# Scaling head 0's probabilities before head 1's decay on VectorE, and copying head 1's first transposes before y on ScalarE

## The chip, the cores and the metric

The kernel runs on one core of a Trainium2 chip (trn2). The metric is the device time of one execution in microseconds (us), given as the median of several runs. The profiled execution is one run of its own, and its span goes from the first to the last instruction.

## The reference

A batch of 8 sequences, each of 36 image tokens and 512 text tokens (548 rows of 192 values), goes through one layer: a normalised attention with decay in 3 heads of 64, and a mixture of 16 experts. Cut to what matters here:

```python
scores = jnp.einsum('blhe,bmhe->bhlm', q, k) / jnp.sqrt(jnp.float32(hd))
decay = jnp.where(mask, gammas[:, None, None] ** dclip, 0.0)   # 0 below the diagonal
weights = jax.nn.softmax(scores * decay[None], axis=-1)
o = jnp.einsum('bhlm,bmhe->blhe', weights, v)
o = (o - mean) / jnp.sqrt(var + GN_EPS)                        # per sequence and head
h = h + (o.reshape(B, L, D) * gn_weight + gn_bias) @ Wo.T
h = h + ffn(layernorm(h))                                      # router, top 8 of 16 experts
```

## The kernel before, in words

Each engine has its own program, written out by hand in the order in which it runs, and the programs meet only at semaphores. There is no scheduler. The attention part goes over the 8 sequences in a function `body(b, ...)` of each engine: b = 0, 1 and 7 are written out, b = 2 to 6 are a loop in hardware. The expert part, `STEPS` steps of up, gelu, weigh, round and down, follows it.

One iteration has three heads. A head passes through four engines. **TensorE** makes the scores (`scores`, L1178) in five row tiles, of which tiles 2 to 4 share PSUM bank 3. **VectorE** multiplies them with the decay table and takes the row maximum (`apply_decay`, L912), and hands the negated maxima on as `nm` (L918), first that of tile 0, after all five tiles those of the other four. **ScalarE** takes the exponentials from the scores `sc` to the probabilities `pr` (`exps`, L598), with the row sums, and an exponential of the maxima alone (`zero_score`, L595), which stands for the positions below the diagonal. VectorE makes the denominators (`den`, L925 and L927), their reciprocals (L929) and scales the five tiles of `pr` in place (`normalise`, L935; tiles of 580, 452, 324, 196 and 68 columns). TensorE transposes the scaled tiles (`probs_transpose`, L1316), in groups 0 to 3, ScalarE copies each group to `pt` (`pt_copy`, L516), and TensorE multiplies with the values (`attend`). Heads 0 and 2 use the buffers `sc[0]` and `pr[0]`, head 1 `sc[1]` and `pr[1]`. So head 1's decay and head 0's scaling touch different buffers.

TensorE's order around the change is: scores of head 1, `values` (the fifth and last tile of which is written to bank 3 and so waits for all of head 1's decay), transposes of head 0, `gn_sums` of the sequence before, `attend` of head 0, transposes 0 and 1 of head 1, scores of head 2, transposes 2 and 3 of head 1, `attend` of head 1.

ScalarE puts head 1's exponentials between its copies of the values, and copies head 0's groups 0 and 1 between the fourth and the fifth exponential. Later it makes y of the sequence before, which waits for coefficients that GpSimd computes (`gn_coefficients`, last instruction L465) from `gvar` (L960). VectorE gets at `gvar` after `gn_partial` (L943 to L950) and head 1's scaling.

**GpSimd** is waiting for `veps` (L828), the last step of the statistics of the next sequence, which VectorE computes between head 0's and head 1's decay. Then it computes `rstd` with a power (L425), two small instructions for `nmr` (L426, L428), and then splits a share of the weights w1: two casts (`w_hi`, L447) and two subtractions (`w_lo`, L450). In b = 7 it splits its share after `second_twice`, instead.

The waits that matter, as the code has them:

```python
# normalise (VectorE)
dve.wait_ge(exp_done, nth(b, H, hh + 1))
# values (TensorE), last tile
if I == NT - 1:
    pe.wait_ge(decayed, nth(b, NT * H, 2 * NT))
# attend (TensorE), before its first matmul
pe.wait_ge(pt_copied, nth(b, 4 * H, 4 * hh + 2))
# probs_transpose (TensorE), groups 2 and 3 of head 1
pe.wait_ge(pt_copied, nth(b, 4 * H, 4 * hh + 1))
# halve_w1 (GpSimd), after rstd_of(b + 1)
pool.wait_ge(ld_w1, nth(b, 16, 16))
```

Of the kernel before, what the change touches and what calls it, by code (L numbers as in the profile page):

```python
# [83 lines left out]
def width(t):  # L84
    return WIDTHS[t]
# [12 lines left out]
def nth(b, per, k):  # L98

    return b * per + k  # L100


def early_fusion(nc, patches, txt, tok_w, tok_b, gammas, gn_w, gn_b, attn_w, w1, w2, out):
# [9 lines left out]
    with ctx:  # L113
# [398 lines left out]
        def _(sc_eng):  # L512
# [90 lines left out]
            def pt_copy(b, hh, groups=(0, 1, 2, 3)):  # L603
                for g in groups:
                    a.wait_ge(pt_done, nth(b, 4 * H, 4 * hh + g + 1))
                    if g == 0:
                        last = copy(pt[:KEY_LAST, 0, :], ps[:KEY_LAST, 5, :])
                    elif g == 1:
                        copy(pt[:KEY_LAST, 1, 0:LAST], ps[:KEY_LAST, 4, 0:LAST])
                        last = copy(pt[:, 1, 64:64 + 3 * P], ps[:, 4, P:4 * P])  # L610
                    elif g == 2:
                        last = copy(pt[:, 2, :], ps[:, 5 if hh else 0, :])
                    else:
                        last = copy(pt[:, 3, 0:3 * P], ps[:, 4 if hh else 1, 0:3 * P])
                    last.then_inc(pt_copied, 1)
# [26 lines left out]
            def logits_exp(t):  # L642
                r = width(t) // SEG
                a.wait_ge(l_sub, t + 1)
                a.activation(lexp[:r, :, :], lsub[:r, :, :], ACT.Exp).then_inc(l_exp, 1)
# [8 lines left out]
            def body(b, tail, later, more):  # L654
                t = b - 1
                qk_round(b, (0,))
                if tail:
                    scale_probs(t)
                qk_round(b, (1, 2, 3))
                if tail:  # L660
                    pt_copy(t, 2)
                if not more:
                    second_norm(0)
                exps(b, 0)
                if tail:
                    o_copy(t, 1)
                if not more:
                    x2_round(0, 0, 4)
                    x2_round(0, 1, 5)
                exps(b, 1, (0,))  # L670
                v_copy(b, (0,))
                exps(b, 1, (1,))
                v_copy(b, (1,))
                exps(b, 1, (2,))
                v_copy(b, (2,))
                exps(b, 1, (3,))
                pt_copy(b, 0, (0, 1))
                exps(b, 1, (4,))
                pt_copy(b, 0, (2, 3))
                if more:  # L680
                    norm_apply(b + 1, rstd, nmr, ln1_rstd, xn, ln1_normed)
                else:
                    logits_exp(0)
                if tail:
                    y_round(t, 0)
                pt_copy(b, 1, (0, 1))
                if tail:
                    y_whole(t, 0)
                    y_round(t, 1)
                pt_copy(b, 1, (2, 3))  # L690
                if tail:
                    y_whole(t, 1)
                exps(b, 2, (0,))
                o_copy(b, 0)
                if more:
                    x_hi(b + 1, 0)
                    x_hi(b + 1, 1)
                    exps(b, 2, (1, 2, 3, 4))
                else:
                    comb_copy(0, 5)  # L700
                    exps(b, 2, (1, 2, 3, 4))
# [89 lines left out]
        def _(dve):  # L791
# [22 lines left out]
            def norm_stats(b, s6, m2, ve, signal):  # L814

                norm_parts(b, s6)
                dve.drain()
                norm_join(s6, m2, ve, signal)
# [79 lines left out]
            def apply_decay(b, hh):  # L898
                s = hh % 2
                for I in range(NT):  # L900
                    r, n = rows(I), L - P * I
                    if I <= 2:
                        dve.wait_ge(s_done, nth(b, 3 * H, 3 * hh + I + 1))
                        apart(dve, "dve")
                    dst, tab = sc[s][:r, OFF[I]:OFF[I] + n], decay[:r, hh, 0:n]
                    if I == 0:
                        dst, tab, src = two(dst), two(tab), ps[:, 0:2, 0:HALF]
                    elif I == 1:
                        src = ps[:, 2, 0:n]
                    else:  # L910
                        src = ps[:r, 3, S_AT[I]:S_AT[I] + n]
                    dve.tensor_tensor_reduce(out=dst, in0=src, in1=tab, scale=1.0 / 8, scalar=0.0 if I else NEG,  # L912
                                             op0=ALU.mult, op1=ALU.max,
                                             accum_out=mx[s][:r, I:I + 1]).then_inc(decayed, 1)
                    if I in (0, NT - 1):
                        dve.drain()
                        cols = slice(0, 1) if I == 0 else slice(1, NT)
                        dve.tensor_scalar(nm[s][:, cols], mx[s][:, cols], -1.0, None, ALU.mult).then_inc(nm_ready, 1)  # L918
# [118 lines left out]
            def body(b, tail, later, more):  # L1037
                t = b - 1
                if isinstance(b, int) and b == 0:
                    dve.wait_ge(ld_h, 16 * NT)  # L1040
                qk_rest(b, (0, 1, 2, 3))
                if not more:
                    second_norm(0)
                if isinstance(b, int) and b == 0:
                    dve.wait_ge(ld_decay, 16)
                    dve.wait_ge(consts, 3)
                apply_decay(b, 0)
                if more:
                    norm_stats(b + 1, st6, mv, veps, ln1_var)
                apply_decay(b, 1)  # L1050
                if not more:
                    x2_rest(0, 0, 4)
                    x2_rest(0, 1, 5)
                normalise(b, 0)
                if tail:
                    gn_partial(t)
                normalise(b, 1)
                if tail:
                    gn_variance(t)
                if not more:  # L1060
                    router_shift(0, 2)
                    router_top(0)
                    router_left(0)
                    router_weights(0)
                apply_decay(b, 2)
                if tail:
                    y_rest(t)
                if more:
                    x_ext(b + 1)
                    x_lo(b + 1, (0,))  # L1070
                    if tail:
                        add_attention(t, (6, 4, 5), (0,))
                    x_lo(b + 1, (1,))
                    if tail:
                        add_attention(t, (6, 4, 5), (1, 2))
                normalise(b, 2)
                if not more:
                    add_attention(t, (4, 3, 5))
# [514 lines left out]
```

## Time and profile before

| what | value |
|---|---|
| median of 3 runs | 849.03 us (848.9 to 854.23) |
| profiled execution | 850.09 us, its span 848.3 us |
| granted TensorE clock, mean | 0.983 of full |
| busy TensorE, VectorE, ScalarE, GpSimd | 805.3, 558.7, 508.2, 101.1 us |
| share of the span | 95%, 66%, 60%, 12% |

The attention part takes the first 320 us or so of the span. One iteration of the hardware loop takes 35.9 us. TensorE is busy for nearly all of both parts, so the time moves only where TensorE waits, or where it begins to.

### The profile page before, as it was taken

The page shows a single profiled execution, that of the slowest core. Times are in us where ns is not written, and L with a number is a line of the kernel's source. Part 1 is how long each engine was busy: PE and PEld are TensorE (multiplying, and loading weights), DVE is VectorE, ACT ScalarE, POOL GpSimd, SP SyncE. Part 2 cuts the span into 40 slices and gives each one's busy share as a digit, 9 for nine tenths or more (in the row PEclk, how much of TensorE's full clock was granted, in tenths as well). Part 3 has the DMA queues.
Part 4 walks back from the last instruction along what each step waited for, and adds up shares of the span by engine and source line. Part 5 has one row for each costly group of instructions (what it writes and reads, how often), then busy time and mean ns, then how long its engine had stood idle before and what let it go on. Part 6 is the DMA issues. An engine that isn't in the chain of part 4 may idle for free.

```text
span 848.3 us, 13687 instructions
## 1 busy us (share of the span) xinstructions
PE 805.3 (95%) x4336; PEld 678.4 (80%) x4336; DVE 558.7 (66%) x1559; ACT 508.2 (60%) x1134; POOL 101.1 (12%) x187
## 2 busy tenths in 40 slices
PE   6799999999999998799999999999999999999997
PEld 2677878797787876677888888888888888888886
DVE  5667677677767777565666666666666566666654
ACT  1367867778777774465555645556555556465443
POOL 2022020220202208300101001001010010000000
PEclk9689999999999999999999999999999999999999
DMA  7400010101103027213422324134133241241420
GB/s 221 152 19 17 5 40 0 38 0 38 38 0 93 1 60 208 79 50 93 120 63 71 106 62 133 41 85 123 53 96 91 68 128 47 80 96 61 113 56 18
DMA packets 44376, 60.77 MB, mean 72 GB/s; under 512 B 4018, under 2 KB 37762, under 8 KB 44322
## 3 DMA queue, kind: packets, MB, share of 16 engines
q1 hardware_dynamic: 44322, 60.10, 25.5%
q8 instruction: 27, 0.44, 0.2%
q14 instruction: 27, 0.22, 0.1%
HBM read 52.04 MB, written 8.05 MB: 71 GB/s over the span
## 4 chain that ended last, share of the span: by engine, by line
PE 61%; issue 26%; POOL 6%; POOLq 3%; DVE 2%; ACT 2%; DVEq 0%; ACTq 0%
PE ps L1178 58%; POOL w_lo L450 2%; POOLq L427 1%; POOL w_lo L482 1%; PE ps L1378 1%; POOLq L460 1%; POOLq L481 1%; POOL w_r L480 0%; PE ps L1316 0%; PE ps L1487 0%; ACT pt L516 0%; PE ps L1488 0%; DVE sc L912 0%; POOLq L448 0%; PE ps L1397 0%
## 5 line engine op out<-in xcount | busy, mean ns | idle before, releaser
L1089 DVE TENSOR_TENSOR act<-act,gate 128x480 f32<-128x480 f32 (+1 forms) x216 | 145.1, 672 | 120.0 <-ACT act L714 118.7
L1178 PE MATMUL ps<-x,w_hi 128*128 128x480 f32 (+1 forms) x648 | 217.4, 390 | 0.0
L714 ACT ACTIVATE act<-ps 128x480 f32<-128x480 f32 (+1 forms) x216 | 124.0, 574 | 125.9 <-PE ps L1178 125.7
L1178 PE MATMUL ps<-x,w_lo 128*128 128x480 f32 (+1 forms) x432 | 165.6, 383 | 0.0
L867 DVE TENSOR_TENSOR act_lo<-act,act_hi 128x480 fp32r<-128x480 f32 (+1 forms) x216 | 144.3, 668 | 0.1
L1178 PEld LDWEIGHTS ps<-x,w_hi 128*128 128x128 f32 x648 | 122.5, 189 | 19.8
L516 ACT ACTIVATE act_hi<-act 128x480 fp32r<-128x480 f32 (+1 forms) x216 | 130.8, 605 | 7.9 <-DVE act L1089 7.9
L1178 PEld LDWEIGHTS ps<-x,w_lo 128*128 128x128 f32 x432 | 81.8, 189 | 13.3
L1178 PE MATMUL ps<-act_hi,w_hi 128*128 128x480 f32 (+1 forms) x216 | 83.9, 388 | 6.6 <-DVE act_lo L867 6.6
L1178 PE MATMUL ps<-act_lo,w_hi 128*128 128x480 f32 (+1 forms) x216 | 83.8, 388 | 0.0
L1178 PE MATMUL ps<-act_lo,w_r 128*128 128x480 f32 (+1 forms) x216 | 83.0, 384 | 0.0
L1178 PE MATMUL ps<-act_hi,w_lo 128*128 128x480 f32 (+1 forms) x216 | 82.8, 384 | 0.0
L1178 PE MATMUL ps<-pt,v 68*128 68x512 f32 (+5 forms) x288 | 82.4, 436 | 0.0
L1178 PE MATMUL ps<-act_hi,w_r 128*128 128x480 f32 (+1 forms) x216 | 82.3, 381 | 0.0
L1178 PEld LDWEIGHTS ps<-pt,v 128*128 128x128 f32 (+1 forms) x288 | 49.0, 190 | 31.1 <-issue 21.6
L598 ACT ACTIVATE pr<-sc,nm 128x580 f32<-128x580 f32 (+4 forms) x120 | 66.8, 559 | 10.7 <-DVE nm L918 10.7
L912 DVE CUSTOM_DVE_ANT_0 sc<-ps,decay 128x548 f32<-128x548 f32 (+4 forms) x120 | 49.7, 458 | 35.5 <-PE ps L1178 33.3
L516 ACT ACTIVATE pt<-ps 128x384 f32<-128x384 f32 (+3 forms) x120 | 48.4, 466 | 23.8 <-PE ps L1316 23.6
L1316 PE MATMUL ps<-ident,pr 128*128 128x128 f32 (+1 forms) x360 | 47.2, 276 | 11.6 <-DVE pr L935 9.1
L425 POOL TENSOR_TENSOR rstdb<-vepsb,neg_half 128x4 f32<-128x4 f32 x9 | 12.2, 1353 | 364.9 <-DVE vepsb L989 364.9
L1178 PEld LDWEIGHTS ps<-act_hi,w_hi 128*128 128x128 f32 x216 | 40.5, 187 | 16.4 <-DVE act_lo L867 9.9
L1316 PEld LDWEIGHTS ps<-ident,pr 128*128 128x128 f32 (+1 forms) x360 | 39.1, 132 | 15.7 <-DVE pr L935 10.9
(173 smaller groups left out, 1318.1 us busy)
## 6 DMA issues: line engine op xcount, KB each, us to landing
gate<-comb_dram SPq DMA_DIRECT2D x112, 240.0 KB, 3.3
gate<-comb_dram SPq DMA_DIRECT2D x32, 256.0 KB, 3.7
w_raw<-w SPq DMA_DIRECT2D x16, 384.0 KB, 3.9
h_dram<-h SPq DMA_DIRECT2D x8, 384.0 KB
res<-h_dram SPq DMA_DIRECT2D x7, 360.0 KB, 4.5
out<-res SPq DMA_DIRECT2D x7, 360.0 KB, 3.2
h<-txt SPq DMA_DIRECT2D x3, 672.0 KB
decay_rows<-drow SPq DMA_DIRECT2D x1, 1014.0 KB, 8.0
```

Source lines behind the costliest of these rows:

```text
L425: pool.tensor_tensor(rs[:, :], ve[:, :], neg_half[:, 0:n], ALU.pow)
L427: pool.drain()
L450: last = pool.tensor_tensor(w1_lo[:, c, cols], w1_raw[:, c, :], w1_hi[:, c, cols], ALU.subtract)
L460: pool.drain()
L516: return a.activation(dst, src, ACT.Copy)
L598: last = a.activation(pr[s][:r, cols], sc[s][:r, cols], ACT.Exp, bias=nm[s][:r, I:I + 1], accum_out=row_sum[s][:r, I:I + 1])
L714: a.activation(act[j % 3][:, 0:n], ps[:, up_bank(j), 0:n], ACT.Gelu_apprx_tanh).then_inc(gelu_done, 1)
L867: return dve.tensor_tensor(dst, src, hi, ALU.subtract)
L912: dve.tensor_tensor_reduce(out=dst, in0=src, in1=tab, scale=1.0 / 8, scalar=0.0 if I else NEG, op0=ALU.mult, op1=ALU.max, accum_out=mx[s][ ...
L1089: dve.tensor_tensor(act[j % 3][:, 0:n], act[j % 3][:, 0:n], gate[e % 4][:, 0:n], ALU.mult).then_inc(gated, 1)
L1178: return pe.matmul(dst, w, x, start=start, stop=stop)
L1316: return pe.transpose(dst, pr[s][:, at:at + n], ident[:, :])
```

## The change

Two pieces of code are moved, and nothing is added or removed. On VectorE `normalise(b, 0)` stands before `apply_decay(b, 1)`. In b = 7 this also puts it before `x2_rest`. On ScalarE the copies of head 1's groups 0 and 1 stand before `y_round(t, 0)`, instead of behind it.

```diff
@@ -681,10 +681,9 @@
                     norm_apply(b + 1, rstd, nmr, ln1_rstd, xn, ln1_normed)
                 else:
                     logits_exp(0)
+                pt_copy(b, 1, (0, 1))
                 if tail:
                     y_round(t, 0)
-                pt_copy(b, 1, (0, 1))
-                if tail:
                     y_whole(t, 0)
                     y_round(t, 1)
                 pt_copy(b, 1, (2, 3))
@@ -1047,11 +1046,11 @@
                 apply_decay(b, 0)
                 if more:
                     norm_stats(b + 1, st6, mv, veps, ln1_var)
+                normalise(b, 0)
                 apply_decay(b, 1)
                 if not more:
                     x2_rest(0, 0, 4)
                     x2_rest(0, 1, 5)
-                normalise(b, 0)
                 if tail:
                     gn_partial(t)
                 normalise(b, 1)
```

All lines behind L684 are one lower in the changed kernel (L935 is L934 there) up to the second piece.

VectorE in the hardware loop, before, from the last step of the statistics on; `sc,mx<-ps,decay` is head 1's decay, of which the first tile and the maxima stand here, and `pr<-pr,inv_den` head 0's scaling:

```order
234 L828 TENSOR_SCALAR veps<-mv 128x5
235 L903 REGISTER_ALU
236 L912 ISA sc,mx<-ps,decay 128x548 [waits s_done]
237 L912 ISA mx 128x1
238 L918 TENSOR_SCALAR nm<-mx 128x1
```

The end of the decay follows eight rows further on, and only then head 0's scaling:

```order
247 L912 ISA sc,mx<-ps,decay 36x36
248 L912 ISA mx 36x1
249 L918 TENSOR_SCALAR nm<-mx 128x4
250 L923 ISA
251 L925 TENSOR_TENSOR den<-zero_score,lower_count 128x5 [waits exp_done]
252 L927 TENSOR_TENSOR den<-den,row_sum 128x5
253 L929 RECIPROCAL inv_den<-den 128x5
254 L935 TENSOR_SCALAR pr<-pr,inv_den 128x580
```

The same place in the changed kernel:

```order
234 L827 TENSOR_SCALAR veps<-mv 128x5
235 L922 ISA
236 L924 TENSOR_TENSOR den<-zero_score,lower_count 128x5 [waits exp_done]
237 L926 TENSOR_TENSOR den<-den,row_sum 128x5
238 L928 RECIPROCAL inv_den<-den 128x5
239 L934 TENSOR_SCALAR pr<-pr,inv_den 128x580
240 L934 TENSOR_SCALAR pr<-pr,inv_den 128x452
241 L934 TENSOR_SCALAR pr<-pr,inv_den 128x324
242 L934 TENSOR_SCALAR pr<-pr,inv_den 128x196
243 L934 TENSOR_SCALAR pr<-pr,inv_den 36x68
244 L902 REGISTER_ALU
245 L911 ISA sc,mx<-ps,decay 128x548 [waits s_done]
```

The wait for `exp_done` now stands directly behind the statistics, and the whole of head 1's decay is queued behind it and behind the eight instructions that follow it.

ScalarE in the written-out iteration b = 1, before, from the normalised x on (`y<-ot` and `ot<-ot` are y, `pt<-ps` the copies of head 1):

```order
95 L546 ACTIVATE xn<-h,nmr,rstd 36x192
96 L626 ACTIVATE y<-ot,gshift,gscale 128x548 [waits y_coeff]
97 L516 ACTIVATE pt<-ps 68x512 [waits pt_done]
98 L516 ACTIVATE pt<-ps 68x36 [waits pt_done]
99 L516 ACTIVATE pt<-ps 128x384
100 L626 ACTIVATE ot<-ot,gshift,gscale 128x548
```

And changed:

```order
95 L546 ACTIVATE xn<-h,nmr,rstd 36x192
96 L516 ACTIVATE pt<-ps 68x512 [waits pt_done]
97 L516 ACTIVATE pt<-ps 68x36 [waits pt_done]
98 L516 ACTIVATE pt<-ps 128x384
99 L626 ACTIVATE y<-ot,gshift,gscale 128x548 [waits y_coeff]
100 L626 ACTIVATE ot<-ot,gshift,gscale 128x548
```

The three copies no longer stand behind the wait for GpSimd's coefficients. The rest of both programs, and those of the other engines, are unchanged.

## Rows read from the trace of the kernel before

**Rows 1.** Waits of TensorE, 40 to 330 us: total us, times, longest us

```profile
PE ps L1316 <- DVE pr L935: 9.1, 7, 1.4
```

**Rows 2.** Timeline of TensorE, loop iteration b = 3: start us, us, ... [idle before]

```profile
156.60 1.83 PE L1316 MATMUL ps<-ident,pr 128*68 128x128 f32 x15 [1.34 <-DVE pr L935]
...
159.12 3.49 PE L1178 MATMUL ps<-pt,v 68*128 68x512 f32 x12
162.44 1.04 PE L1316 MATMUL ps<-ident,pr 128*68 128x128 f32 x8
...
165.01 1.01 PE L1316 MATMUL ps<-ident,pr 128*128 128x128 f32 x7
```

**Rows 3.** Timeline of VectorE, the same iteration

```profile
150.93 0.73 DVE L912 CUSTOM_DVE_ANT_0 sc<-ps,decay 128x548 f32<-128x548 f32 x1 [1.64 <-PE ps L1178]
...
153.46 0.87 DVE L918 TENSOR_SCALAR nm<-mx 128x4 f32<-128x4 f32 x1
154.24 0.15 DVE L925 TENSOR_TENSOR den<-zero_score,lower_count 128x5 f32<-128x5 f32 x1
...
154.97 1.57 DVE L935 TENSOR_SCALAR pr<-pr,inv_den 128x580 f32<-128x580 f32 x5
...
161.64 0.17 DVE L960 TENSOR_SCALAR gvar<-gvar 128x2 f32<-128x2 f32 x1
```

**Rows 4.** Timeline of ScalarE, the same iteration

```profile
149.86 0.19 ACT L598 ACTIVATION_READ_ACCUMULATOR pr<-sc,nm 36x1 f32 x1
...
151.95 0.78 ACT L598 ACTIVATE pr<-sc,nm 128x580 f32<-128x580 f32 x1 [1.34 <-DVE nm L918]
...
154.36 0.21 ACT L595 ACTIVATE zero_score<-nm 128x5 f32<-128x5 f32 x1 [0.18 <-DVE nm L918]
...
157.27 1.06 ACT L516 ACTIVATE pt<-ps 68x512 f32<-68x512 f32 x3 [0.20 <-PE ps L1316]
...
163.63 0.84 ACT L626 ACTIVATE y<-ot,gshift,gscale 128x548 fp32r<-128x548 f32 x1 [1.94 <-POOL gshift L465]
164.38 1.03 ACT L516 ACTIVATE pt<-ps 68x512 f32<-68x512 f32 x3
```

**Rows 5.** Timeline of GpSimd, the same iteration

```profile
149.37 1.19 POOL L425 TENSOR_TENSOR rstd<-veps,neg_half 128x5 f32<-128x5 f32 x1 [21.28 <-DVE veps L828]
...
150.87 0.20 POOL L428 TENSOR_TENSOR nmr<-nmr,rstd 128x5 f32<-128x5 f32 x1
151.15 0.95 POOL L447 CAST w_hi<-w_raw 128x384 f32 x2
152.31 1.99 POOL L450 TENSOR_TENSOR w_lo<-w_raw,w_hi 128x384 f32 x2 [0.21 <-issue]
```

**Rows 6.** VectorE grouped by shape, 118.9 to 120.7 us: busy us, mean ns | idle

```profile
L935 DVE TENSOR_SCALAR pr<-pr,inv_den 128x580 f32<-128x580 f32 x1 | 0.5, 523 | 0.1
...
L935 DVE TENSOR_SCALAR pr<-pr,inv_den 128x196 f32<-128x196 f32 x1 | 0.3, 316 | 0.0
```

**Rows 7.** VectorE grouped by shape, 317.4 to 320.3 us (head 2 of b = 7)

```profile
L935 DVE TENSOR_SCALAR pr<-pr,inv_den 128x196 f32<-128x196 f32 x1 | 1.1, 1078 | 0.0
```

**Rows 8.** VectorE grouped by shape, 44 to 50.2 us (b = 0)

```profile
L927 DVE TENSOR_TENSOR den<-den,row_sum 128x5 f32<-128x5 f32 x1 | 1.0, 1018 | 0.1
L935 DVE TENSOR_SCALAR pr<-pr,inv_den 128x580 f32<-128x580 f32 x1 | 0.9, 922 | 0.1
```

**Rows 9.** Timeline of GpSimd, expert part: a power like that of `rstd`

```profile
740.26 1.38 POOL L425 TENSOR_TENSOR rstdb<-vepsb,neg_half 128x4 f32<-128x4 f32 x1 [49.83 <-DVE vepsb L989]
```

**Rows 10.** VectorE grouped by shape, 739.5 to 742 us

```profile
L1089 DVE TENSOR_TENSOR act<-act,gate 128x480 f32<-128x480 f32 x2 | 1.3, 656 | 0.0
```

**Rows 11.** Page, part 5: the whole group of the same line: busy, mean ns | idle

```profile
L1089 DVE TENSOR_TENSOR act<-act,gate 128x480 f32<-128x480 f32 (+1 forms) x216 | 145.1, 672 | 120.0 <-ACT act L714 118.7
```

**Rows 12.** Timeline of VectorE, b = 7

```profile
294.69 0.73 DVE L912 CUSTOM_DVE_ANT_0 sc<-ps,decay 128x548 f32<-128x548 f32 x1 [2.68 <-PE ps L1178]
```

**Rows 13.** Timeline of ScalarE, b = 7

```profile
295.52 0.19 ACT L598 ACTIVATION_READ_ACCUMULATOR pr<-sc,nm 36x1 f32 x1
```

## The prediction

> **What bounds the kernel now.** I read the page first: TensorE is busy for nearly all of the span, so only its waits can be won. The list of waits, cut to the attention part, has one large entry: the transposes of head 0 wait for VectorE's scaling 7 times, 9.1 us in all [rows 1]. All numbers below are from the timelines of one iteration of the hardware loop, b = 3. The reader is to see three things there. TensorE idles 1.34 us ahead of the transposes [rows 2], because the scaling, which starts at 154.97, is queued behind head 1's decay [rows 3]. Head 0's exponentials were already done at 149.86 + 0.19 = 150.05 [rows 4], and VectorE idled 1.64 us before 150.93 [rows 3]. So the work could be done in the gap, in part. And GpSimd works exactly in that stretch: 149.37 to 154.30 [rows 5].
>
> **First edit, what it moves.** From the first `den` to the first `pr` it is 154.97 - 154.24 = 0.73 us, and the five scalings take 1.57 us: 2.30 us [rows 3]. Started at 150.09 (150.05 and 0.04 for the semaphore) they would end at 152.39, undisturbed. Head 1's decay then starts not at 150.93 but at about 152.38. Call its delay d; it is at least 1.45 us.
>
> **What is queued behind it.** Everything on ScalarE up to head 0's copies hangs on that decay. Before, `zero_score` started at 154.36, 3.43 us after the decay's start. Of this 0.70 us was the second `nm`, which took 0.87 where others of its shape take 0.17. It now falls behind GpSimd's work, so 2.73 us remain. From `zero_score` to the end of the copies of groups 0 and 1 it is 157.27 + 1.06 - 154.36 = 3.97 us, of which 0.20 us was a wait for the transposes [rows 4]. These are earlier now, so 3.77 us remain. The copies end at 150.93 + d + 2.73 + 3.77 = 157.43 + d, and `attend` starts 0.04 us later, at 157.47 + d. Before it started at 159.12 [rows 2]. So TensorE's **shift at `attend` is d - 1.65 us**. Even with d = 1.45 the gain is 0.2 us out of the 1.34 us of the wait: ScalarE becomes the bound. I take this chain as the latest because the others are earlier. The last tile of `values` waits for the decay's end at about 150.93 + d + 2.35, takes 0.6 us, and the transposes take 1.83 us: 155.8 + d. `gn_partial`, moved up behind the decay, takes 2.3 us (three quarters of it the four instructions at L943), and ends near 155.9 + d. Head 1's scaling starts when its exponentials are done, near 157.8 + d, and ends at 160.1 + d, ahead of the transposes of head 1, which come 162.44 - 159.12 = 3.32 us after `attend` [rows 2], at 160.8 + d.
>
> **Second edit.** TensorE's last transposes of head 1 start at 165.01, 2.57 us after the first [rows 2]. Scores of head 2 fill all of that but about 0.25 us, in which TensorE waits for the first copy, which was queued behind y at 164.38 [rows 4]. Now the copies start as soon as the transposes are done. This gives back 0.25 us per iteration. y itself waits for `gshift`, which released it at 163.63 [rows 4] and lies on VectorE's chain through `gvar` at 161.64 [rows 3]. y's three instructions then follow the copies and groups 2 and 3 are copied about as late relative to TensorE as before, so I cost this at nothing; if that cover fails it is up to 0.3 us per iteration. **The shift of an iteration is d - 1.9 us**: a gain below 1.9, a loss above it.
>
> **The size of d: GpSimd.** The rows show VectorE stopped by GpSimd. The second `nm`, four values wide, took 0.87 us and ended at 154.33; GpSimd's `w_lo` ended at 154.30 [rows 3, 5]. `den`, five wide, took 1018 ns beside one `w_lo` of b = 0, and the scaling of 580 columns 922 ns where 523 ns is its own time [rows 8, 6]. A scaling of 196 columns took 1078 ns instead of 316 [rows 7, 6] beside the splitting of w2. In all of these VectorE's instruction ended just after GpSimd's. The decay shows none of it. So I take it that the two engines take turns, instruction by instruction, whoever asks first, when VectorE scales within SBUF or reads two operands there. The new place of the scaling, 150.8 to 152.4, lies on GpSimd's two casts (151.15, 0.48 us each) and runs into its two subtractions (152.31, 1.0 us each) [rows 5].
>
> The turns, worked out: first scaling from 151.02 (behind `nmr`) to 151.32; cast until 151.71; second scaling until 151.94; cast until 152.33; third scaling until 152.50. The fourth asks at 152.635, since VectorE needs 0.13 us between two (5 durations that sum to 1.91 us lie within 1.57 us, and 523 ns at the front holds some 0.16 us before the data). The first `w_lo` asks at about 152.66: GpSimd has 0.21 us idle there [rows 5] and some 0.07 us at its start. **If the fourth scaling is first**, it is done at 152.74, `w_lo` holds until 153.68, and the fifth ends at 153.78: d = 2.77. **If `w_lo` is first**, the fourth and the fifth wait for one `w_lo` each and end at 154.74: d = 3.75. The two are 25 ns apart by estimates that are no better than 50 ns. I take the first, since the sum puts it there.
>
> The Trainium skill has a rule for this (SBUF — State Buffer, section Who interferes with whom): VectorE's scaling instructions from SBUF to SBUF and its instructions with two SBUF inputs share a port pair with GpSimd, and whichever "starts first gets the pair for the whole instruction; the other fully blocks". By that rule the trace agrees in every row named above, and it speaks against this change.
>
> **The sum.** Loop iterations, b = 2 to 6: 5 x (2.77 - 1.9) = +4.4 us. b = 1, written out: GpSimd has no pause before its casts there, the first cast comes before the first scaling, and the same turns give d = 3.65. Its gain from the copies is 0.37 us instead of 0.25, but y comes too late and takes that back: +2.1 us. b = 0: the exponentials are done 0.2 us after the statistics, the scaling gets ahead of the subtractions, d = 2.96. There is no y, and TensorE, at the transposes' end at 52.17, was less far ahead of ScalarE: +1.2 us. b = 7: the decay started at 294.69, but the exponentials are done at only 295.71 [rows 12, 13]; the first `den` waits for `w_lo` until 296.5, the scaling ends at 298.7, d = 4.0. Behind it stand `x2_rest` (1.4 us), the router's logits and the transposes; the copies and VectorE's router chain come 2.6 to 2.9 us later, and the copies ahead of y give some back: +2.7 us. Sum: 4.4 + 2.1 + 1.2 + 2.7 = **+10.4 us**. Made against the profiled execution, 850.1 us, this gives 860.5; its time is 1.1 us above the median, so against the median of 849.03 it is **859.4 us**, 1.2% slower. The expert part is unchanged and only starts later.
>
> **The rivals.**
>
> *w_lo wins the draw in the loop.* For it: the 25 ns. Then 5 x (3.75 - 1.9) = 9.3 in place of 4.4: +15.3 us, 864.3 us.
>
> *The power holds the pair too.* If GpSimd's power stops VectorE as its subtractions do, the first `den`, asked at 150.09, waits for `rstd` until 150.56 [rows 5], everything starts 0.45 us later, both `w_lo` fall between scalings, and d is 4.0. That is 5 x 2.1 = 10.5 for the loop and 6.5 for the other three: +17 us, 866 us. Against it: beside the power at 740.26 VectorE's two instructions with two SBUF inputs took 656 ns on average, and the whole group has a mean of 672 [rows 9 to 11]. This rival is what the same section of the Trainium skill's page SBUF — State Buffer gives, which speaks of whole instructions and makes no difference between kinds of them; the rows of the power do not agree with it.
>
> *No collision.* The tiles of the scaling may slip in between GpSimd's instructions, since only 0.3 us of the largest is data. d is 1.45 and the loop gains 5 x 0.45 = 2.3 us, b = 1 gains 0.4, b = 0 still loses 0.7 and b = 7, whose exponentials come late, 2.0. The sum is zero: 849 us. Against it: a waiting VectorE was stopped each time [rows 3, 7, 8].
>
> *The other side: the gain in full.* If ScalarE could take the later start of head 1's exponentials from its idle time (1.34 us before 151.95 [rows 4]), TensorE would win the 9.1 us of waits [rows 1] and 7 x 0.25 less b = 0 at the copies, 1.5 us: 838.4 us, faster. It decides at d below 0.3 or so in my chain, that is, if the scaling were done almost when the decay used to start, at 150.93. Since it starts at 150.09 and takes 2.30 us, I see no way but a wrong chain: ScalarE's copies of the values would have to hide the delay, and they stand in line with the exponentials, with 0.18 to 0.70 us of idle between them.
>
> **How the numbers follow.** Turns, fourth scaling first: 0.40. `w_lo` first: 0.25. The power as well: 0.06. No collision: 0.20. The gain in full: 0.05. Anything else: 0.04. The likeliest gives 859.4. The range, 847 to 866, leaves out the gain in full and little more. A measurement of this kernel can tell about 1% from no change, 8.5 us: slower is above 857.5, and that holds 0.7 of the first case (its own range is 855 to 862), all of the second and third, a little of the rest: 0.61. Faster than 840.5 only the full gain: 0.06. Same: 0.33.
>
> **What would show it.** In the profile after, TensorE's wait for `pr` at the transposes of head 0 is gone or small. In its place are a wait at the fifth tile of `values` for the decay, 1 to 2 us per iteration, and one at `attend` for ScalarE's `pt`. The five scalings of head 0 take 2.8 to 4 us instead of 1.57, with single ones near 0.7 or 1.1 us, while those of head 1 stay at 1.57; GpSimd's casts are stretched by 0.2 to 0.3 us. The loop's period rises from 35.9 to about 36.8 us (37.8 if `w_lo` is first, 35.5 without a collision). The transposes of head 1, groups 2 and 3, start 2.32 instead of 2.57 us after groups 0 and 1. The prediction is wrong if the scalings take 1.6 us beside GpSimd, or if `attend` starts much less than 6.5 us after head 1's decay does.

## The result, and the profile after

The changed kernel is slower: 864.02 us (median of 4 runs, 863.58 to 864.94), beside 849.0 us for the kernel before (median of 4 runs: 848.9, 848.96, 849.03 and 854.23). The ratio on record is 1.0142, with a 95% interval of 1.011 to 1.0174; it isn't the quotient of the two medians, which is 1.0177. The median is 4.6 us above the forecast of 859.4. The kernel before scatters more than the changed one: its 57 runs beside the experiments lie between 848.26 and 856.36 us, with a median of 853.03, so against that median the changed kernel is 11 us slower and not 15. (One more run of it, beside experiments 1 to 4, was in a slow state at 2019.67 us and is left out.) The profiled execution took 863.58 us with a span of 861.8, so the spans differ by 13.5 us (861.8 - 848.3).

The page of the changed kernel, parts 1 and 2 (busy time, share, instructions; the granted clock in 40 slices):

```profile
PE 812.0 (94%) x4336; PEld 682.9 (79%) x4336; DVE 566.5 (66%) x1559; ACT 507.6 (59%) x1134; POOL 102.8 (12%) x187
...
PEclk9699999999999999999999999999999999999999
```

The page says little: TensorE is as full as before. The list of waits, cut to the attention part (40 to 345 us), says what changed (total us, times, longest):

```profile
PE ps L1177 <- DVE mx L911: 15.0, 8, 4.0
...
PE ps L1177 <- ACT pt L516: 5.0, 6, 1.0
...
PE ps L1177 <- DVE gmv L949: 0.9, 5, 0.2
```

The wait of the transposes for `pr`, 9.1 us in 7 pieces [rows 1], is gone from it, and that for `gmv` was 3.3 us in 7 pieces before. Two others stand in its place: the last tile of `values` waits for head 1's decay (its row is named by `mx`, the decay's second output), and `attend` waits for ScalarE's copies `pt`.

The timeline of TensorE, in the two loop iterations b = 2 and b = 3, and the same product in b = 5 and b = 6. It answers to [rows 2]:

```profile
122.79 0.33 PE L1177 MATMUL ps<-aw_hi,xa_hi 128*68 128x256 f32 x1 [1.43 <-DVE mx L911]
...
126.75 3.50 PE L1177 MATMUL ps<-pt,v 68*128 68x512 f32 x12 [0.97 <-ACT pt L516]
130.09 1.04 PE L1315 MATMUL ps<-ident,pr 128*68 128x128 f32 x8
...
132.37 0.98 PE L1315 MATMUL ps<-ident,pr 128*128 128x128 f32 x7
...
159.36 0.33 PE L1177 MATMUL ps<-aw_hi,xa_hi 128*68 128x256 f32 x1 [1.42 <-DVE mx L911]
...
161.98 0.35 PE L1177 MATMUL ps<-gmv,head_mean 128*128 128x4 f32 x2 [0.19 <-DVE gmv L949]
163.31 5.19 PE L1177 MATMUL ps<-pt,v 68*128 68x512 f32 x12 [0.97 <-ACT pt L516]
168.34 1.04 PE L1315 MATMUL ps<-ident,pr 128*68 128x128 f32 x8
...
238.15 5.08 PE L1177 MATMUL ps<-pt,v 68*128 68x512 f32 x12 [0.98 <-ACT pt L516]
...
276.37 5.19 PE L1177 MATMUL ps<-pt,v 68*128 68x512 f32 x12 [0.97 <-ACT pt L516]
```

The reader is to see two things. The waits are the same in both iterations, 1.42 to 1.43 and 0.97 us. But the twelve matmuls of `attend` behind them take 3.50 us in b = 2 and 5.19 us in b = 3. (That of b = 5 is as slow as the others, though its row says 5.08: from the start of the product to the end of the eight transposes behind it, b = 3, 5 and 6 all take 6.07 us, b = 2 and 4 take 4.38.) The windows view of the same stretches tells why (us, busy time and count of PE, PEld, DVE, ACT, POOL, then granted clock, DMA share, GB/s):

```profile
126.70:130.20 3.50, 3.45 (x14) 2.18 (x15) 2.66 (x12) 3.37 (x9) 0.00 (x0) 1.00 0.02 5
...
159.36:163.30 3.94, 2.79 (x22) 2.49 (x22) 2.21 (x9) 3.69 (x15) 0.00 (x0) 1.00 0.77 207
163.30:168.50 5.20, 5.19 (x14) 3.04 (x15) 2.66 (x12) 3.33 (x9) 1.26 (x4) 0.67 0.00 0
168.50:172.00 3.50, 3.50 (x30) 3.25 (x28) 1.72 (x6) 3.02 (x6) 0.46 (x2) 1.00 0.00 0
```

A granted clock of 0.67 is a mix of the two levels: if f is the part at 2.4 GHz, f + 0.5 (1 - f) = 0.67 gives f = 0.34, so 3.4 of the 5.2 us passed at 1.2 GHz. They cost half of that, 1.7 us, and 5.19 - 3.50 = 1.69. What follows starts again at 1.00.

The timeline of VectorE in b = 3, which answers to [rows 3]:

```profile
152.41 0.17 DVE L827 TENSOR_SCALAR veps<-mv 128x5 f32<-128x5 f32 x1
153.38 0.17 DVE L924 TENSOR_TENSOR den<-zero_score,lower_count 128x5 f32<-128x5 f32 x1 [0.80 <-ACT pr L598]
...
154.13 2.84 DVE L934 TENSOR_SCALAR pr<-pr,inv_den 128x580 f32<-128x580 f32 x5
156.89 0.71 DVE L911 CUSTOM_DVE_ANT_0 sc<-ps,decay 128x548 f32<-128x548 f32 x1
...
159.40 0.17 DVE L917 TENSOR_SCALAR nm<-mx 128x4 f32<-128x4 f32 x1
...
164.37 1.57 DVE L934 TENSOR_SCALAR pr<-pr,inv_den 128x580 f32<-128x580 f32 x5
```

Head 0's five scalings take 2.84 us, head 1's 1.57. The decay starts 156.89 - 152.41 = 4.48 us after `veps`. GpSimd of the same stretch [rows 5]:

```profile
152.66 1.18 POOL L425 TENSOR_TENSOR rstd<-veps,neg_half 128x5 f32<-128x5 f32 x1 [20.26 <-DVE veps L827]
...
154.43 1.21 POOL L447 CAST w_hi<-w_raw 128x384 f32 x2
155.85 2.04 POOL L450 TENSOR_TENSOR w_lo<-w_raw,w_hi 128x384 f32 x2 [0.21 <-issue]
```

And VectorE by shape, 154.0 to 157 us (busy us, mean ns):

```profile
L934 DVE TENSOR_SCALAR pr<-pr,inv_den 36x68 f32<-36x68 f32 x1 | 1.0, 998 | 0.0
L934 DVE TENSOR_SCALAR pr<-pr,inv_den 128x452 f32<-128x452 f32 x1 | 0.7, 687 | 0.0
L934 DVE TENSOR_SCALAR pr<-pr,inv_den 128x324 f32<-128x324 f32 x1 | 0.6, 624 | 0.0
L934 DVE TENSOR_SCALAR pr<-pr,inv_den 128x580 f32<-128x580 f32 x1 | 0.5, 536 | 0.1
L934 DVE TENSOR_SCALAR pr<-pr,inv_den 128x196 f32<-128x196 f32 x1 | 0.3, 307 | 0.0
```

In the order of the program they are 580, 452, 324, 196 and 68 columns wide. The first is free, the second and third wait for a cast each, the fourth is free, and the fifth, the smallest, waits for a whole `w_lo`. These are the turns that the prediction worked out, in its case "the fourth scaling is first".

**Where the 13.5 us are.** I took the starts of `rstd` on GpSimd as marks, one in each iteration. From mark to mark, after less before: b = 0 33.30 to 34.43, +1.1; b = 1 35.96 to 37.75, +1.8. In b = 2 to 5 the period was 35.97, 35.93, 35.97 and 35.93; it is now 36.57, 38.26, 36.57 and 38.24 (from 116.09, 152.66, 190.92 and 227.49 on). The long ones hold a slow product, and so does b = 6. So an iteration grows by 0.63 us, and by another 1.68 us where the clock falls. For b = 2 to 6 that is 5 x 0.63 + 3 x 1.68 = 3.2 + 5.0 = 8.2 us. b = 7 up to the split of w2 takes 31.16 instead of 28.14 us, +3.0. The sum is 14.1; the stretches before and behind give back 0.6.

### The profile page after: what moved, and what is told of

Same layout as the page of the kernel before. It is cut to its first block, busy times and chain, and to the rows that moved or that the text cites. A ratio compares the mean times of both kernels' runs of the same rounds, so it can differ in the third digit from the quotient of the medians.

```text
span 861.8 us, 13687 instructions
## 1 busy us (share of the span) xinstructions
PE 812.0 (94%) x4336; PEld 682.9 (79%) x4336; DVE 566.5 (66%) x1559; ACT 507.6 (59%) x1134; POOL 102.8 (12%) x187
## 4 chain that ended last, share of the span: by engine, by line
PE 78%; ACT 6%; DVE 5%; issue 5%; POOL 3%; POOLq 1%; DVEq 1%; ACTq 0%
PE ps L1177 71%; PE ps L1315 4%; ACT pr L598 3%; DVE pr L934 2%; DVE sc L911 2%; POOL w_lo L482 1%; ACT pt L516 1%; PE ps L1215 1%; PE ps L1377 1%; DVEq L915 1%; POOLq L481 1%; PE ps L1486 0%; PE ps L1487 0%; POOL w_r L480 0%; ACT v L516 0%
## 5 line engine op out<-in xcount | busy, mean ns | idle before, releaser
L1177 PE MATMUL ps<-pt,v 68*128 68x512 f32 (+5 forms) x288 | 87.8, 457 | 5.0 <-ACT pt L516 5.0
L1177 PEld LDWEIGHTS ps<-pt,v 128*128 128x128 f32 (+1 forms) x288 | 51.4, 199 | 39.4 <-issue 25.4
L1315 PE MATMUL ps<-ident,pr 128*128 128x128 f32 (+1 forms) x360 | 50.6, 290 | 0.9 <-DVE h L973 0.8
L1177 PEld LDWEIGHTS ps<-act_lo,w_r 128*128 128x128 f32 x216 | 40.6, 188 | 8.0
```

Of the source, the lines that this page charges most:

```text
L1177: return pe.matmul(dst, w, x, start=start, stop=stop)
L1315: return pe.transpose(dst, pr[s][:, at:at + n], ident[:, :])
```

## The experiments

None of the edits changes what is computed. The ratio is always to runs of the kernel before that were made beside the experiment. Their median was 852.07 us (first four experiments), 851.25 (the fifth), 853.03 (sixth to eighth) and 853.91 (the last two), so absolute times from different rows of the table aren't compared here. "Period" is the time between starts of `rstd` in b = 2 to 5, in the one profiled execution of each kernel. Line numbers shift by one or two from kernel to kernel.

| kernel | ratio, 95% interval | median us | period, us |
|---|---|---|---|
| changed kernel | 1.0142, 1.011 to 1.0174 | 864.02 | 36.57, 38.26, 36.57, 38.24 |
| first edit alone | 1.0171, 1.0141 to 1.0201 | 866.02 | 37.62, 37.60, 37.60, 37.60 |
| second edit alone | 0.9969, 0.994 to 0.9999 | 848.99 | 35.68, 35.63, 35.67, 35.63 |
| changed, split later | 1.0042, 1.0021 to 1.0063 | 855.78 | 36.97, 37.01, 35.34, 36.98 |
| before, split later | 1.0151, 1.0119 to 1.0182 | 864.68 | 37.83, 37.02, 37.83, 37.80 |
| changed, with fillers | 1.0100, 1.0062 to 1.0139 | 860.13 | 36.59, 36.58, 36.59, 36.58 |
| split later, with fillers | 0.9970, 0.9951 to 0.9988 | 850.24 | 35.31, 35.34, 35.36, 35.31 |
| second edit, split first | 0.9885, 0.9832 to 0.9938 | 843.69 | 34.99, 34.98, 35.00, 34.97 |
| changed, split first | 1.0038, 1.0017 to 1.0059 | 855.76 | 36.97, 37.00, 35.30, 37.00 |
| second edit, split first, sums inside `attend` | 0.9856, 0.9823 to 0.989 | 839.73 | 34.51, 34.53, 34.50, 34.50 |
| changed, split first, fillers | 0.9968, 0.9955 to 0.9982 | 850.99 | 35.31, 35.31, 35.31, 35.35 |

### 1. The first edit alone

```
                 if more:
                     norm_stats(b + 1, st6, mv, veps, ln1_var)
+                normalise(b, 0)
                 apply_decay(b, 1)
...
-                normalise(b, 0)
```

> Only the first edit (VectorE's order). The theory that the loss comes from the delay of head 1's decay and all that hangs on it: as slow as the full change or 1 to 2 us slower, 864 to 866 us, since the copies of head 1 again stand behind y (0.25 us per iteration). The rival that ScalarE's new order costs the time: near 849 us.

Measured: 1.0171. The period is 37.6 us and no product of the loop is slow. TensorE waits as in the changed kernel, and once more, for the copies ahead of the last transposes (timeline of TensorE, b = 2):

```profile
127.64 3.50 PE L1178 MATMUL ps<-pt,v 68*128 68x512 f32 x12 [0.97 <-ACT pt L516]
...
134.27 1.01 PE L1316 MATMUL ps<-ident,pr 128*128 128x128 f32 x7 [0.85 <-ACT pt L516]
```

So the first edit alone carries the loss, without any slow product in the loop. The copies of head 1, which stand behind y here, wait with it for a later `gshift`; the wait of about 0.25 us became 0.85.

### 2. The second edit alone

```
+                pt_copy(b, 1, (0, 1))
                 if tail:
                     y_round(t, 0)
-                pt_copy(b, 1, (0, 1))
-                if tail:
                     y_whole(t, 0)
```

> Only the second edit (ScalarE's order). The first theory: 1.5 to 3 us faster than before (0.25 us in five iterations, 0.4 and 0.6 in b = 1 and 7), 846 to 847.5 us, with the transposes of groups 2 and 3 of head 1 2.32 us behind groups 0 and 1 instead of 2.57. The rival that y, now later, costs the time: slower than 855 us.

Measured: 0.9969; its 10 runs lie between 845.87 and 853.35 us, and the profiled one, at 846.22, is among the fastest. The verdict rests on its period, 35.63 to 35.68, which is 0.3 us less than before. The term of 0.25 us was right for this edit by itself. Beside the first edit it is worth more, 37.60 - 36.58 = 1.02 us: the two do not add.

### 3. The changed kernel without the collision

GpSimd's split of the weights waits until head 1's decay is over:

```
             def halve_w1(b):
+                pool.wait_ge(decayed, nth(b, NT * H, 2 * NT))
```

> The changed kernel, in which GpSimd begins its split of w1 only after all of head 1's decay, so that it no longer runs beside head 0's scaling. Theory of turns between GpSimd and VectorE: the five scalings take 1.57 us again, head 1's decay starts 2.3 us instead of 3.5 us after the end of head 0's exponentials, an iteration of the loop takes about 35.4 us, and the time is 846 to 850 us. The rival that the mere place of the scaling in VectorE's queue costs the time, or that ScalarE's later exponentials do whatever GpSimd does: 860 us or more. A second theory adds that part of the loss (three loop iterations with a product that takes 5.19 instead of 3.50 us) is TensorE's clock after its waits: it should go with the waits.

Measured: 1.0042. VectorE and GpSimd in b = 4 (one timeline each):

```profile
190.40 1.60 DVE L935 TENSOR_SCALAR pr<-pr,inv_den 128x580 f32<-128x580 f32 x5
191.93 0.71 DVE L912 CUSTOM_DVE_ANT_0 sc<-ps,decay 128x548 f32<-128x548 f32 x1
...
196.47 0.40 DVE L948 TENSOR_TENSOR gtmp<-gmv 128x2 f32<-128x2 f32 x1
...
196.94 0.88 DVE L950 TENSOR_TENSOR gmv<-gmv,gtmp 128x2 f32<-128x2 f32 x1
```

```profile
195.85 1.96 POOL L451 TENSOR_TENSOR w_lo<-w_raw,w_hi 128x384 f32 x2 [0.21 <-issue]
```

The scalings are back at 1.60 us, so GpSimd was what stretched them. Two things went against my expectation of 846 to 850 us. `w_lo` now lies on the two small instructions of the group norm, and one of them, two columns wide, takes 0.88 us where it took 0.16 before: it ends at 197.82, `w_lo` at 197.81. And three of the four periods are 37.0 us because of the clock:

```profile
160.96 0.35 PE L1178 MATMUL ps<-gmv,head_mean 128*128 128x4 f32 x2 [1.12 <-DVE gmv L950]
161.34 5.19 PE L1178 MATMUL ps<-pt,v 68*128 68x512 f32 x12
```

Ahead of this slow product there is one wait of over 1 us, and not two: that at the last tile of `values` is 0.17 us here.

### 4. The kernel before, with the same wait

```
             def halve_w1(b):
+                pool.wait_ge(decayed, nth(b, NT * H, 2 * NT))
```

> The kernel before with the same wait for GpSimd. If turns are what stretches the second nm to 0.87 us, that nm takes 0.17 us and the scaling starts 0.7 us earlier: about 0.6 us in each of six iterations, 845 to 846 us. If the long nm is no matter of GpSimd: 849 us.

Measured: 1.0151, a clear miss. In the order of before, head 0's scaling comes right behind the decay, so the wait moved the split onto that scaling. TensorE's waits over 40 to 345 us, and one of them in the timeline:

```profile
PE ps L1317 <- DVE pr L936: 19.0, 8, 3.4
```

```profile
129.08 3.26 PE L1317 MATMUL ps<-ident,pr 128*68 128x128 f32 x15 [2.43 <-DVE pr L936]
...
166.91 1.83 PE L1317 MATMUL ps<-ident,pr 128*68 128x128 f32 x15 [2.43 <-DVE pr L936]
```

The wait for `pr` grew from 9.1 to 19.0 us, in the loop from 1.34 to 2.43 an iteration. In b = 2, 4 and 5 the transposes behind it ran slow as well, 3.25 to 3.38 us instead of 1.83; in b = 3 they didn't, and that period is 0.8 us shorter. So 1.1 of the 1.9 us by which a long period grew is the wait, and 0.8 us is TensorE's clock. My error was to look only at where the split had been. But the run shows the collision from the other side: with the order of before and the split on the scaling, a loss of the same size comes back.

### 5. The changed kernel with fillers

To see what TensorE's clock costs, dead matmuls (their results are never read) fill its waits. They read operands that already lie in SBUF:

```
                     if I == NT - 1:
+                        if more:
+                            for _ in range(12):
+                                mm(ps[:, 5, 0:256], xa_hi[:, 0:P], ah, True, True)
                         pe.wait_ge(decayed, nth(b, NT * H, 2 * NT))
...
+                if more:
+                    for _ in range(8):
+                        mm(ps[:, 3, 0:256], xa_hi[:, 0:P], aw_hi[:, 0, QK_W:QK_W + V_W], True, True)
                 attend(b, 0)
```

> The changed kernel, with matmuls whose result nobody reads put into TensorE's two new waits in b = 0 to 6: 12 of 256 columns before the fifth tile of values, 8 before attend of head 0 (0.12 us each, 1.4 and 0.9 us, the size of the waits). The outputs are the same. Theory that some 5 to 8 us of the loss are TensorE's clock, which falls to its lower level after the waits: no product of head 0 takes 5.19 us, the granted clock is 1.00 throughout the loop, and the time is 856 to 860 us. The rival that the slow products have another cause, or that the clock falls anyway: 864 us or more, by as much as the fillers hold up TensorE.

Measured: 1.0100. The period is 36.58 us in all four, as in the undisturbed iterations of the changed kernel. `attend` in b = 3:

```profile
161.71 0.36 PE L1177 MATMUL ps<-gmv,head_mean 128*128 128x4 f32 x2 [0.19 <-DVE gmv L949]
...
163.04 3.50 PE L1177 MATMUL ps<-pt,v 68*128 68x512 f32 x12
```

This separates the two losses in the loop: 36.58 - 35.95 = 0.63 us in every iteration is the change itself, the rest is clock. The ratio falls by 0.42 points, 3.6 us; the intervals of the two ratios (1.0062 to 1.0139, 1.011 to 1.0174) overlap a little, so here the verdict rests on the periods. The fillers stand in b = 0 to 6 only; in b = 7 the transposes of head 0 are still slow (3.41 us).

### 6. Split later, with fillers

Experiment 3 with nine of the fillers ahead of `gn_sums`, and with them TensorE's wait for ScalarE's copies of the values (`v_copied`), which stood behind `gn_sums`.

> The changed kernel with the split behind head 1's decay, as in the third run, and 9 matmuls whose result nobody reads in TensorE's wait for gmv in b = 0 to 6 (0.12 us each, 1.1 us). In the third run the loop took 35.34 us where the product behind that wait ran at full clock and 37.0 where it took 5.19 us (three times). If the clock after the wait is the cause, all loop iterations take 35.3 to 35.4 us and the time is 849 to 852 us. The rival, that something else makes the product slow: 855 us or more.

Measured: 0.9970, period 35.31 to 35.36. Without the collision on the scaling and without the loss of clock, the changed order would be about as good as its second edit alone.

### 7. The second edit, with the split in front

The order of before on VectorE, but GpSimd splits first:

```
             def body(b, tail, later, more):
+                halve_w1(b)
...
                     rstd_of(b + 1, ln1_var, rstd, mv, veps, nmr, ln1_rstd)
-                halve_w1(b)
```

> ScalarE's edit alone, and GpSimd splits its share of w1 at the front of its iteration, behind the last copy of the iteration before, so beside head 2's decay and y's remainder. If turns with GpSimd cost the old order 0.7 us at the second nm, the scaling starts 0.7 us earlier, the loop takes 35.0 to 35.1 us instead of 35.65, and the time is 841 to 844 us. If that nm was not on TensorE's path: 846 us, as with ScalarE's edit alone. If the turns only cost the same elsewhere (the nm of head 2, y): above 847.

Measured: 0.9885, period 34.97 to 35.00. The second `nm` no longer waits for `w_lo` (it takes 0.17 us), and the wait for `pr` falls from 1.34 to 0.73 us. Beside it the wait for `gmv` stands as it did; first its row in the kernel before, b = 3, then experiment 7:

```profile
158.90 0.36 PE L1178 MATMUL ps<-gmv,head_mean 128*128 128x4 f32 x2 [0.47 <-DVE gmv L950]
```

```profile
156.15 1.83 PE L1315 MATMUL ps<-ident,pr 128*68 128x128 f32 x15 [0.73 <-DVE pr L934]
...
158.45 0.36 PE L1177 MATMUL ps<-gmv,head_mean 128*128 128x4 f32 x2 [0.48 <-DVE gmv L949]
```

So nearly half of the old wait was a matter of GpSimd, and this half could be had without touching VectorE's order. Of the 1.15% the second edit has 0.3; the split in front has the rest (0.9885 / 0.9969 = 0.992).

### 8. The changed kernel, with the split in front

The same move in the changed kernel.

> The changed kernel with GpSimd's split in that same place. The scaling is free of turns and so is gn_partial: the five scalings take 1.57 us, gn_sums waits 0.2 us or less, and by the shift of d - 1.77 at attend, less 0.25 at the copies, the loop takes 35.2 to 35.4 us at full clock. If that is all, 844 to 847 us; if TensorE's clock falls in some iterations after its remaining waits, up to 852 us. If the order of VectorE is bad by itself: above 855.

Measured: 1.0038, a median of 855.76 us. That misses the expectation: it is above the 852 us that I allowed for the clock, and in the place that I had given to "the order of VectorE is bad by itself". Part of that is the level of these runs, in which the kernel before took 853.03 us and not 849; experiment 10 tells the rest. The scalings take 1.59 us, and the waits at `values` and at `gn_sums` are 0.17 and 0.18. The period at full clock is 35.30 us, as expected. But one product is slow again in three of the four periods and in b = 6, and this behind a single wait of 0.97 us and two of under 0.2; b = 3 and b = 4 differ in nothing that I can see ahead of it:

```profile
160.50 5.19 PE L1177 MATMUL ps<-pt,v 68*128 68x512 f32 x12 [0.97 <-ACT pt L516]
...
197.51 3.50 PE L1177 MATMUL ps<-pt,v 68*128 68x512 f32 x12 [0.97 <-ACT pt L516]
```

### 9. The best version

Experiment 7, and the group norm's sums, which waited 0.48 us for `gmv`, moved behind the third of `attend`'s six multiplications in the code (the sixth of the twelve matmuls in the trace):

```
                 probs_transpose(b, 0)
-                if tail:
-                    gn_sums(t)
                 pe.wait_ge(v_copied, nth(b, 3, 3))
-                attend(b, 0)
+                attend(b, 0, between=(lambda: gn_sums(t)) if tail else None)
```

> The fastest so far (ScalarE's edit, GpSimd's split first) with gn_sums moved from before attend of head 0 to between its third and fourth matmul. If the 0.47 us that TensorE waits for gmv per iteration is on its path, the loop takes 34.5 to 34.6 us instead of 34.99 and the time is 840 to 842 us, 2 to 3 us below the 843.7 of that kernel; the rival, that attend then waits for ScalarE's copies instead, or y comes later and group 2 of head 1 with it: 843 to 845 us.

Measured: 0.9856, period 34.50 to 34.53. It is the fastest of all, by the ratio 1.4% below the kernel before and 2.8% below the changed one (0.9856 / 1.0142 = 0.972). Only the wait for `pr` is left in this part of the loop:

```profile
151.30 1.83 PE L1315 MATMUL ps<-ident,pr 128*68 128x128 f32 x15 [0.73 <-DVE pr L934]
```

### 10. The changed kernel, split in front, with fillers

Experiment 8 with one filler ahead of the last tile of `values` and eight ahead of `attend`.

> The changed kernel with GpSimd's split first and fillers in TensorE's waits, 1 before the fifth tile of values and 8 before attend of head 0. Without the fillers the loop took 35.30 us where the product of head 0 took 3.50 us and 36.98 where it took 5.19 (four times in b = 2 to 6), and the time was 855.8 us. If the clock after the wait is the cause, the loop takes 35.3 us throughout and the time is 847 to 850 us; otherwise 855 us or more.

Measured: 0.9968, period 35.31 to 35.35, every product of head 0 in the loop at 3.50 us:

```profile
157.71 3.50 PE L1177 MATMUL ps<-pt,v 68*128 68x512 f32 x12
```

So 0.7 points of experiment 8 were clock. What remains is the price of the order itself: 35.31 against 34.98 in experiment 7, where VectorE keeps the order of before. With the split out of the way of both orders and the clock held up, the first edit still loses 0.3 us an iteration. The profiled spans, 847.5 and 843.5 us, differ by 4.0; the loop makes 1.7 of that, and the rest lies in b = 0, 1 and 7.

## Why the prediction was right, and where it was short

**What bounds the kernel: right.** The wait for `pr` was the one that the first edit removes, and it vanished; the decay of head 1 and ScalarE's chain behind it took its place, as forecast. The first edit alone (experiment 1) shows the loss.

**The turns with GpSimd: right.** d was forecast as 2.77 us. Before, the decay came 150.93 - 149.12 = 1.81 us after the start of `veps`, the last step of the statistics; now 4.48: d = 2.67. The five durations are those of the case that was taken over its rival by 25 ns, and the fifth took 998 ns. That this draw fell on the right side is partly luck: the prediction itself called its estimates no better than 50 ns. Experiments 3 and 8 took GpSimd away and the scalings took 1.59 to 1.60 us. By the section on who interferes with whom in the Trainium skill (SBUF — State Buffer), the pair of ports is held for a whole instruction; the casts and `w_lo` agree with that, the smallest scaling, 998 ns, most plainly. (The words that the prediction quotes stand in another section of that page, SBUF: two separate sides. The section on who interferes also tells GpSimd instructions that read SBUF from those that only write it; the power reads it, so that doesn't take it out of the rule.) The rival in which the power holds it as well didn't happen: `den` started at 153.38 and took 0.17 us, while `rstd` ran from 152.66 to 153.84.

**The chain behind the decay: right.** `attend` starts 163.31 - 156.89 = 6.42 us after head 1's decay; 6.54 was forecast. The last transposes follow 2.28 us after the first (132.37 - 130.09), 2.32 was forecast. Signs that the prediction named, the wait of 1 to 2 us at the last tile of `values`, the one for `pt`, the casts stretched by 0.26 us (1.21 instead of 0.95), all stand in the profile.

**The terms of the sum.** Mechanical growth of an iteration: 0.63 us against 0.87. The three small differences above, 0.10, 0.12 and 0.04, come to 0.26 and so explain the 0.24. For the loop that is 3.2 instead of 4.4 us. b = 0 was 1.1 (forecast 1.2), b = 1 1.8 (2.1), b = 7 3.0 (2.7). In the first two the transposes of head 0, behind waits for the decay of 3.98 and 2.18 us, ran slow, 2.75 and 3.21 us instead of 1.83; that lies in time in which TensorE would have waited for `pt` anyway, since `attend` starts 6.44 and 6.46 us after the decay, as in the loop. In b = 7 it doesn't. There `attend` starts 318.07 - 309.41 = 8.66 us after the decay, and in experiment 8, where the same transposes ran at full clock, 309.48 - 302.25 = 7.23. First the changed kernel, then experiment 8 (TensorE, b = 7):

```profile
314.77 3.23 PE L1315 MATMUL ps<-ident,pr 128*68 128x128 f32 x15
```

```profile
307.61 1.83 PE L1315 MATMUL ps<-ident,pr 128*68 128x128 f32 x15
```

So about 1.4 of the 3.0 us of b = 7 are clock too, an estimate, since experiment 8 also moves the split. With b = 7 as measured these terms give 858.1 us (849.0 + 3.2 + 1.1 + 1.8 + 3.0), without its clock 856.7. That is growth of 7.7 us where 10.4 were forecast: the mechanical part was forecast 2.7 us too high.

**The term that was missing: TensorE's clock.** The sum, "+10.4 us", has none. Three products of the loop took 5.19 instead of 3.50 us, 5.0 us in all: 858.1 + 5.0 = 863.1. With the 1.4 us of b = 7 the term is about 6.4 us. The 2.7 us too much and the 6.4 us too little partly cancel, so the distance of 4.6 us makes the sum look better than it was, which is luck.

The rest up to 864.0 is the difference between profiled execution and median (850.1 and 849.0 before, 863.58 and 864.02 after: 1.5 us) less the 0.6 us at the two ends.

I removed one wait of 1.34 us and put two in its place, of 1.43 and 0.97 us, and didn't ask what this does to the clock of the matmuls behind them. That it is the pair that matters is not shown: in experiment 8 a single wait of 0.97 us stood ahead of four slow products, and in the profiled execution of the kernel before waits of 1.34 and 0.47 us stood ahead of none. The page of the kernel before had a hint, a granted clock of 0.6 in its second slice (21 to 42 us), where TensorE has a wait of 5.93 us; but in its loop the products took 3.5 us, and I took that for granted. The fillers (experiments 5, 6 and 10) show the size of this term in the loop. The kernel before may not be free of it either: of its 57 runs the nine below 850 us have a mean granted clock of 0.983, the 18 above 854 us one of 0.980. Only an execution of 850.09 us was profiled, so where the others lose time is not shown, and neither is how much of the 13.5 us would be left beside a slower execution.

**A number that was right for another reason.** The rival "*w_lo wins the draw in the loop*" gave 864.3 us, almost the measured time. Its mechanism did not happen: the periods would have been 37.8 us in all iterations, and the fourth scaling would have waited for a `w_lo`. Experiment 5 rules it out as well.

**The weighing of the edits.** The second edit was costed by itself, 0.25 us, and subtracted. By itself it was worth 0.3 us, beside the first edit 1.0 us. The forecast stood because d - 1.65 assumed copies that don't wait behind y. With the first edit alone the same formula would have given 35.95 + 2.67 - 1.65 = 36.97, and 37.6 was measured.

**What stays open.** Why TensorE's clock falls in b = 3, 5 and 6 and not in b = 2 and 4, with the same waits ahead. In experiment 1 the same three waits (1.44, 0.19 and 0.97 us) brought no slow product in the loop at all. The Trainium skill (TensorE: Matmul & The Clock Gate, section What's actually happening) says that the gate lets all or half of the pulses through, depending on how busy the engine has been; the two durations fit that, but no run here shows what decides between two iterations that look alike. So the forecast of such a term would have been a range: nothing, to 1.69 us in each of five iterations, 8.5 us.

## What to carry to other kernels

Before work is moved into a gap of one engine, look at what another engine does in that gap: here GpSimd's split of the weights lay just there, and the five scalings took 2.84 instead of 1.57 us. Here the cheaper edit was to move that other work: the split moved to the front of GpSimd's body gave 0.8% with VectorE's order left alone, while moved behind the decay it cost 1.5%, since it fell on head 0's scaling, for which TensorE waits.

When a change moves, lengthens or adds waits of about 1 us on TensorE, add a term for the clock of the matmuls behind them, as a range that starts at nothing. Here it was 5.0 us in the loop, and about 6.4 of the 13.5 us with the last iteration.

## What the runs showed that I had not expected

- The same waits give a product of 3.50 or of 5.19 us, with a granted clock of 1.00 or 0.67, in neighbouring iterations of one execution; in the changed kernel the pattern is b = 3, 5 and 6, with the split in front b = 2, 3, 5 and 6.
- Nine to twenty matmuls whose results nobody reads, put into the waits of an iteration, made the kernel faster: 1.0042 to 0.9970 and 1.0038 to 0.9968, with intervals apart, and 1.0142 to 1.0100, with intervals that overlap.
- An instruction two columns wide took 0.88 us (`gmv` beside `w_lo`, experiment 3), and one on 68 columns 998 ns. That they are small did not protect them.
